# One graph and mixer layer on one core: centring moved to GpSimd, small constants moved behind the last tile, the mixing matrix made by halves

## What is computed

```python
xn  = layernorm(x)
xt  = xn @ weight                                  # graph branch: 4 heads of 64
alpha = softmax(leaky_relu(al[src] + ar[dst]))     # first N edges only
gnn = repeat(sum_h alpha[:, h] * xt[dst][:, h], 4)
q, k, v = split(xn @ w_qkv.T)                      # mixer branch: 8 heads of 64
k, v = instance_norm(k), instance_norm(v)
dots = k.T @ v                                     # per head, 64 x 64, over all rows
mix  = (q @ dots / N) @ w_out.T + b_out
x = x + gnn + mix
x = x + moe(layernorm(x))                          # router, top 2 of 6 experts, 3 layers each
```

## Time and profile before

| what | value |
|---|---|
| median of 3 runs | 802.78 us (802.03 to 805.83) |
| profiled execution | 807.41 us |
| its span, first to last instruction | 805.6 us |
| mean granted TensorE clock | 0.936 of full speed |
| busy: PE, DVE, ACT, POOL | 84%, 69%, 55%, 50% |

### The profile page before, as it was taken

One profiled execution on the slowest core, in us unless ns is written; L12 is line 12 of the kernel. 1 busy time (PEld: TensorE's weight loads), 2 busy tenths in 40 slices (PEclk: granted clock), 3 DMA queues, 4 the chain that ended last, 5 costly groups with the idle time before them and its releaser, 6 DMA issues.

```text
span 805.6 us, 15446 instructions
## 1 busy us (share of the span) xinstructions
PE 679.5 (84%) x4744; PEld 625.0 (78%) x4744; DVE 557.4 (69%) x1401; ACT 442.0 (55%) x873; POOL 398.9 (50%) x439
## 2 busy tenths in 40 slices
PE   3867999999999678878861599999994799999992
PEld 2867888888888567777741499999994799999992
DVE  5676579898888557767746277677773377777772
ACT  2545566777777236756740466556651566565640
POOL 3436378877666000443637045555555145555553
PEclk9989999999999799999955699999998699999997
DMA  8784645444443434764234434343432524545420
GB/s 230 158 166 119 158 126 142 134 126 140 128 121 87 155 118 143 238 191 155 71 99 129 121 117 140 130 140 133 131 120 84 166 88 127 147 124 137 134 73 29
DMA packets 72463, 106.24 MB, mean 132 GB/s; under 512 B 24612, under 2 KB 45605, under 8 KB 72386
## 3 DMA queue, kind: packets, MB, share of 16 engines
q1 hardware_dynamic: 51074, 72.57, 31.9%
q0 software_dynamic: 21312, 32.69, 13.4%
HBM read 60.32 MB, written 46.78 MB: 133 GB/s over the span
## 4 chain that ended last, share of the span: by engine, by line
PE 76%; ACT 6%; DVE 5%; DMA 4%; issue 4%; POOL 3%; SPq 1%; POOLq 0%; DVEq 0%; ACTq 0%
PE kv_ps L1303 10%; PE kv_ps L1305 10%; PE kv_ps L1304 10%; PE pt L1295 6%; PE d_ps L1174 5%; PE kv_ps L1151 5%; PE kv_ps L1154 4%; PE kv_ps L1152 4%; PE kv_ps L1238 3%; PE xt_ps L1295 3%; POOL tab L553 2%; PE pt L1229 2%; PE pt L1154 2%; PE pt L1151 2%; PE pt L1152 2%
## 5 line engine op out<-in xcount | busy, mean ns | idle before, releaser
L1303 PE MATMUL kv_ps<-we_h,now_h 128*128 x648 | 198.1, 306 | 13.9 <-issue 8.3
L1305 PE MATMUL kv_ps<-we_h,now_l 128*128 x648 | 185.5, 286 | 0.0
L1304 PE MATMUL kv_ps<-we_l,now_h 128*128 x648 | 184.9, 285 | 0.0
L1303 PEld LDWEIGHTS kv_ps<-we_h,now_h 128*128 128x128 f32 x648 | 125.6, 194 | 19.6 <-issue 19.6
L1304 PEld LDWEIGHTS kv_ps<-we_l,now_h 128*128 128x128 f32 x648 | 125.4, 194 | 0.0
L1305 PEld LDWEIGHTS kv_ps<-we_h,now_l 128*128 128x128 f32 x648 | 124.7, 193 | 0.0
L1099 DVE TENSOR_TENSOR work<-kv_ps,be 128x256 f32<-128x256 f32 x216 | 81.6, 419 | 45.0 <-PE kv_ps L1305 41.1
L564 POOL TENSOR_TENSOR arena<-work,arena 128x256 f32<-128x256 f32 x80 | 53.1, 683 | 109.2 <-ACT work L730 109.2
L524 POOL DMA_INDIRECT alg<-al_tab,src_all x50 | 62.1, 1243 | 41.9 <-issue 28.1
L914 DVE TENSOR_REDUCE ss<-xring 125x16 f32<-125x1040 f32 x50 | 61.7, 1234 | 20.3 <-ACT xring L635 17.7
L527 POOL DMA_INDIRECT arena<-xt_tab,dst_all x50 | 61.8, 1236 | 15.2 <-issue 15.2
(11 more groups left out here) (238 smaller groups left out, 1832.1 us busy)
## 6 DMA issues: line engine op xcount, KB each, us to landing
arena<-tab SPq DMA_DIRECT2D x40, 259.0 KB
xring<-in_x SPq DMA_DIRECT2D x26, 224.0 KB
xt_tab<-arena SPq DMA_DIRECT2D x10, 568.8 KB
arena<-tab SPq DMA_DIRECT2D x40, 131.0 KB
we_h<-wt_h SPq DMA_DIRECT2D x6, 768.0 KB
we_l<-wt_l SPq DMA_DIRECT2D x6, 768.0 KB
weight_in<-tab SPq DMA_DIRECT2D x14, 259.0 KB
xring<-in_x SPq DMA_DIRECT2D x5, 560.0 KB
```

The lines of the kernel that those rows point to most:

```text
L1303: pe.matmul(outp, hi[:, c, :], we_h[:, w], start=c == 0, stop=False)
L1304: pe.matmul(outp, hi[:, c, :], we_l[:, w], start=False, stop=False)
L1305: last = pe.matmul(outp, lo[:, c, :], we_h[:, w], start=False, stop=c == KC - 1)
```

## The change

It has four parts.

- **Centring.** VectorE keeps the sum and the multiplication of `centre`; the four additions become `kv_centre` on GpSimd, after tiles 29, 31, 33 and 35, each with a wait on `mean_done`. ScalarE's casts move from pairs 14 and 16 to pairs 17 and 19.
- **Small constants.** `small` moves from pair 20 to behind the last pair. The product of zeros that needs its last two areas moves on TensorE from before the first key product to behind the first value product. VectorE and ScalarE wait for it at tile 2.
- **Diagonal copies.** VectorE copies the diagonal blocks first, then does the two `weights` pieces of the last chunk, and the three `graph` pieces and `graph_rows(0)` after one more step.
- **Mixing matrix by halves.** The four first products go into two banks and signal by pairs; ScalarE scales the first half and VectorE the second; the eight products that follow are run by halves of the sum; the two column blocks of the result lie in banks of their own, and are rounded (ScalarE) and lowered (VectorE) one after the other.

The diff, without the declarations of semaphores:

```diff
-PREP_EPS, PREP_BO, PREP_W = 1, 15, 20
+PREP_EPS, PREP_BO, PREP_W = 1, 13, 18
+        a_ps = [kv_ps[0][:, 2 * D * b:2 * D * (b + 1)].rearrange("p (b n) -> p b n", b=2) for b in range(2)]
+        m_ps = [kv_ps[1][:, 512 * c:512 * c + D] for c in range(KC)]
@@ gpsimd
+            def kv_centre(part):
+                half, c = part // 2, part % 2
+                cols = slice(half * MI, half * MI + MI)
+                kv_v = kv_raw[:, c, cols].rearrange("p (h n) -> p h n", n=MC)
+                pool.wait_ge(mean_done, half + 1)
+                pool.tensor_tensor(kv_v, kv_v, kv_mean[:, c, half * MH:half * MH + MH].unsqueeze(2).to_broadcast([128, MH, MC]),
+                                   ALU.add).then_inc(kv_c, 1)
             for t in range(T):
                 normal(t)
+                if t >= 29 and t % 2 == 1 and t < 37:
+                    kv_centre((t - 29) // 2)
                 if t >= 40 and t % 2 == 1 and t < 48:
                     kv_lower((t - 40) // 2)
@@ scalar
-                if i in (14, 16):
-                    half = (i - 14) // 2
+                if i in (17, 19):
+                    half = (i - 17) // 2
-                    act.wait_ge(kv_c, half + 1)
+                    act.wait_ge(kv_c, KC * (half + 1))
+                if t == 2:
+                    act.wait_ge(dz_done, 1)
             act.wait_ge(a_done, 1)
-            act.activation(a_sb, kv_ps[0][:, :].rearrange("p (b n) -> p b n", b=MI // 128), ACT.Copy,
-                           scale=1.0 / N).then_inc(as_done, 1)
+            act.activation(a_sb[:, 0:2, :], a_ps[0], ACT.Copy, scale=1.0 / N).then_inc(as_first, 1)
             for b in range(2):
                 act.wait_ge(cv_out[b], 16 * ROUNDS)
-            act.wait_ge(m_done, 1)
-            act.activation(mix_h, xt_ps[:, :].rearrange("p (c n) -> p c n", c=KC), ACT.Copy).then_inc(mh_done, 1)
+            for c in range(KC):
+                act.wait_ge(m_done, c + 1)
+                act.activation(mix_h[:, c, :], m_ps[c], ACT.Copy).then_inc(mh_done, 1)
@@ vector
-                link(dve.tensor_scalar(mean_v, mean_v, -1.0 / MC, None, ALU.mult))
-                for c in range(KC):
-                    last = dve.tensor_tensor(kv_v[:, c, :, :], kv_v[:, c, :, :], mean_v[:, c, :].unsqueeze(2).to_broadcast([128, MH, MC]), ALU.add)
-                last.then_inc(kv_c, 1)
+                dve.tensor_scalar(mean_v, mean_v, -1.0 / MC, None, ALU.mult).then_inc(mean_done, 1)
-                if i == 20:
-                    small()
-            dve.wait_ge(prep, PREP_W)
+            small()
-            for q in range(5):
+            dve.wait_ge(dT_done, 1)
+            dve.wait_ge(dots_done, T)
+            d_v = d_ps[:, :].rearrange("p (b n) -> p b n", b=MI // 128)
+            for q in range(2):
+                dve.tensor_copy(dotsT[MC * q:MC * (q + 1), :, MC * q:MC * (q + 1)],
+                                d_v[MC * q:MC * (q + 1), :, MC * q:MC * (q + 1)]).then_inc(dT_done, 1)
+            for q in range(2):
+                piece(CHUNKS - 1, q)
+            dve.wait_ge(a_done, 2)
+            dve.tensor_scalar(a_sb[:, 2:4, :], a_ps[1], 1.0 / N, None, ALU.mult).then_inc(as_done, 1)
+            for q in range(2, 5):
                 piece(CHUNKS - 1, q)
             graph_rows(0)
...
-            dve.wait_ge(mh_done, 1)
-            dve.tensor_tensor(mix_l, xt_ps[:, :].rearrange("p (c n) -> p c n", c=KC), mix_h.bitcast(FP32), ALU.subtract).then_inc(ml_done, 1)
+            for c in range(KC):
+                dve.wait_ge(mh_done, c + 1)
+                dve.tensor_tensor(mix_l[:, c, :], m_ps[c], mix_h[:, c, :].bitcast(FP32), ALU.subtract).then_inc(ml_done, 1)
@@ tensor
-            pe.wait_ge(prep, PREP_W)
-            pe.matmul(d_ps[:, :], vs[2][:, 0:128], ks[2], start=True, stop=False, skip_group_check=True)
...
+                if t == 0:
+                    pe.wait_ge(prep, PREP_W)
+                    pe.matmul(d_ps[:, :], vs[2][:, 0:128], ks[2], start=True, stop=False, skip_group_check=True).then_inc(dz_done, 1)
...
-            for q in range(MI // 128):
-                last = pe.matmul(kv_ps[0][:, q * D:(q + 1) * D], dotsT[:, q, :], woT_sb[:, q, :], start=True, stop=True)
-            last.then_inc(a_done, 1)
+            for b in range(2):
+                for q in range(2):
+                    last = pe.matmul(a_ps[b][:, q, :], dotsT[:, 2 * b + q, :], woT_sb[:, 2 * b + q, :], start=True, stop=True)
+                last.then_inc(a_done, 1)
+            def mix_weights(c, b):
+                for q in (2 * b, 2 * b + 1):
+                    last = pe.matmul(m_ps[c], wq_sb[:, q, c * 128:(c + 1) * 128], a_sb[:, q, :],
+                                     start=q == 0, stop=q == MI // 128 - 1)
+                return last
+            pe.wait_ge(as_first, 1)
+            for c in range(KC):
+                mix_weights(c, 0)
             pe.wait_ge(as_done, 1)
-            for c in range(KC):
-                for q in range(MI // 128):
-                    last = pe.matmul(xt_ps[:, c * D:(c + 1) * D], wq_sb[:, q, c * 128:(c + 1) * 128], a_sb[:, q, :],
-                                     start=q == 0, stop=q == MI // 128 - 1)
-            last.then_inc(m_done, 1)
-            pe.wait_ge(ml_done, 1)
+            for c in range(KC):
+                mix_weights(c, 1).then_inc(m_done, 1)
+            pe.wait_ge(ml_done, KC)
```

More of the change, by code:

```diff
@@ L257, in gps_layer @@
         wg_c, wg_hd, wg_ld = sem("wg_c"), sem("wg_hd"), sem("wg_ld")
-        kv_c, kv_hd, kv_ld = sem("kv_c"), sem("kv_hd"), sem("kv_ld")
+        mean_done, kv_c, kv_hd, kv_ld = sem("mean_done"), sem("kv_c"), sem("kv_hd"), sem("kv_ld")
         bs_done, ag_done, sd_done, fin_done = sem("bs_done"), sem("ag_done"), sem("sd_done"), sem("fin_done")
@@ L265, in gps_layer @@
                                                           sem("pr_done"), sem("sr_done"))
-        rc_done, ks_ready, dots_done = sem("rc_done"), sem("ks_ready"), sem("dots_done")
+        rc_done, ks_ready, dz_done, dots_done = sem("rc_done"), sem("ks_ready"), sem("dz_done"), sem("dots_done")
         g_in = [sem(f"g_in{b}") for b in range(2)]
@@ L271, in gps_layer @@
         cvh_done, cvl_done = sem("cvh_done"), sem("cvl_done")
-        dT_done, a_done, as_done, m_done, mh_done, ml_done = (sem("dT_done"), sem("a_done"), sem("as_done"),
+        dT_done, a_done, as_first, as_done, m_done, mh_done, ml_done = (sem("dT_done"), sem("a_done"), sem("as_first"), sem("as_done"),
                                                               sem("m_done"), sem("mh_done"), sem("ml_done"))
@@ L923, in _ @@
                 dve.wait_ge(rc_done, t + 1)
+                if t == 2:
+                    dve.wait_ge(dz_done, 1)
                 if t >= VB:
@@ L950, in _ @@
             graph_rows(0)
-            dve.wait_ge(dT_done, 1)
-            dve.wait_ge(dots_done, T)
-            d_v = d_ps[:, :].rearrange("p (b n) -> p b n", b=MI // 128)
-            for q in range(2):
-                dve.tensor_copy(dotsT[MC * q:MC * (q + 1), :, MC * q:MC * (q + 1)],
-                                d_v[MC * q:MC * (q + 1), :, MC * q:MC * (q + 1)]).then_inc(dT_done, 1)
-            dve.wait_ge(mh_done, 1)
-            dve.tensor_tensor(mix_l, xt_ps[:, :].rearrange("p (c n) -> p c n", c=KC), mix_h.bitcast(FP32), ALU.subtract).then_inc(ml_done, 1)
+            for c in range(KC):
+                dve.wait_ge(mh_done, c + 1)
+                dve.tensor_tensor(mix_l[:, c, :], m_ps[c], mix_h[:, c, :].bitcast(FP32), ALU.subtract).then_inc(ml_done, 1)
             dve.wait_ge(pool_c, POOL_C)
@@ L1196, in _ @@
             pe.wait_ge(dT_done, 3)
-            for q in range(MI // 128):
-                last = pe.matmul(kv_ps[0][:, q * D:(q + 1) * D], dotsT[:, q, :], woT_sb[:, q, :], start=True, stop=True)
-            last.then_inc(a_done, 1)
+            pe.wait_ge(ks_ready, T)
+            pe.wait_ge(sqv_done, T)
+            for b in range(2):
[7 more added lines that the diff above has]
+                return last
+            pe.wait_ge(vs_ready, T)
+            pe.wait_ge(as_first, 1)
+            for c in range(KC):
+                mix_weights(c, 0)
             pe.wait_ge(as_done, 1)
             for c in range(KC):
-                for q in range(MI // 128):
-                    last = pe.matmul(xt_ps[:, c * D:(c + 1) * D], wq_sb[:, q, c * 128:(c + 1) * 128], a_sb[:, q, :],
-                                     start=q == 0, stop=q == MI // 128 - 1)
-            last.then_inc(m_done, 1)
-            pe.wait_ge(ml_done, 1)
+                mix_weights(c, 1).then_inc(m_done, 1)
+            pe.wait_ge(ml_done, KC)
             def mix(i):
```

## The result

| | before | after |
|---|---|---|
| median of 12 runs | 804.09 us (802.03 to 808.06) | 798.49 us (792.89 to 802.37) |
| ratio, 95% interval | | 0.9918 [0.9897, 0.9940] |
| profiled execution, its span | 807.41 us, 805.6 us | 797.89 us, 795.7 us |
| last dots end / mixing starts | 269.44 / 286.50 | 268.95 / 278.56 |

The account below looks back on a forecast made before the run. TensorE, busy 84%, was taken to lose time in the passage behind stage 2 and at the end of stage 1. Gains of 8.85 + 3.15 = 12.0 us from 802.8 gave 790.8 us, range 786.5 to 796.5.

Parts of the forecast that it names:

- stage 1 net: End of stage 1: gain of 3.6 us less 0.45 us for the product of zeros, 3.15 us (2.5 to 3.8).
- passage: Behind stage 2, from last dots to mixing: TensorE starts the mixing at 277.65 instead of 286.50, gain 8.85 us.
- mixing loop: The loop after the passage, untouched by the diff; the forecast's sum had no term for it.
- If all upstream comes earlier, the store does too: Stage 1: the store releasing ScalarE's table copy ahead of the cast also comes earlier, 1.3 us allowed; gain 4.25 us.
- The centring's upstream saving: Stage 1: VectorE gives up 1.29 us of additions twice, ScalarE some 1.0 us of casts twice; 1.3 us allowed.
- The taken 3.6 us: Stage 1 gain before the product of zeros, taken as the middle between 2.95 and 4.25 us.
- The price of an addition: Each centring addition on GpSimd: taken as 1.3 us, bounded by 0.65 and 2.6 us, hidden in idle time.
- stage 1 gives nothing: Rival, 9%: stage 1 is bound by its transfers and the constants only filled a hole; 794.0 us.
- The rival of the clock: Rival, 18%: TensorE's clock still falls in the passage, about 3 us of the gain is lost; 793.8 us.
- The rival of the loop: Rival, 7%: the mixing loop's first row and bias loads come late, half of 8.85 us is lost; 795.2 us.
- GpSimd as the bound: Rival, 2%: additions and normalisations between tiles 29 and 36 bind; whole gain gone at 5.5 us per addition.
- The thin cover of the constants: End of stage 1: 4.5 us of constants against 5.0 us until TensorE wants the zeros; TensorE waits for any tenths missed.

Follow-up runs that it names:

- e9: Changed kernel with the centring additions back on VectorE and the casts behind pairs 14 and 16; 795.01 us, 0.9926 of the kernel before.
- e14: Changed kernel with casts at pairs 15 and 16 and extra products in TensorE's two waits of the mixing loop; 793.95 us, 0.9870 of the kernel before.
- e16: Kernel before with only the diagonal copies and mixing matrix by halves changed, a second time; 797.57 us, 0.9914 of the kernel before.
- e11: The changed kernel itself, run a third time; 795.73 us, 0.9925 of the kernel before.
- e5: Changed kernel with the casts at pairs 15 and 16 instead of 17 and 19; 794.31 us, 0.9886 of the kernel before.
- e8: Changed kernel with casts at pairs 15 and 16 and extra TensorE products during the wait for the diagonal copies; 794.23 us, 0.9887 of the kernel before.
- e10: Changed kernel with the casts at pairs 15 and 16, a second time; 794.03 us, 0.9899 of the kernel before.
- e3: The changed kernel itself, run a second time; 796.00 us, 0.9912 of the kernel before.

## Why the prediction was wrong

The direction and the order of the passage were right, the size was not. By its own steps, with means over all profiles:

| step | forecast | measured |
|---|---|---|
| stage 1 net | 3.15 us | 1.0 us (268.59 - 267.58) |
| passage | 8.85 us | 7.4 us (16.00 over six - 8.58 over twelve) |
| mixing loop | 0 | -1.4 us (130.9 - 132.3) |
| sum | 12.0 us | 7.0 us; by the medians 5.6, 7.0 and 6.7 us |

- *"If all upstream comes earlier, the store does too": this step of stage 1 failed, and with it the forecast that only GpSimd's queue waits for the late cast.* I had named the danger (the cast moved behind a copy that a store releases) and set bounds of 2.95 and 4.25 us on it, but both assumed that the store lands no later against the rest than before. In the profile after it was issued 1.95 us earlier and released ScalarE 0.8 us later (0.95 us earlier and 0.85 us later in the means from the mark), so the cast ended at 68.4, outside both cases. I allowed 1.3 us for busy transfers; they took it all. And the sum followed the cast to GpSimd alone, while ScalarE's `upper` of the next pair stands behind the same wait and the same cast: TensorE stood for 2.0 to 3.0 us for it in all five profiles of the changed stage 1, and in four of them ran at half clock afterwards. With the casts ahead of the wait stage 1 gains 2.8 us (3.0 from the mark), inside the forecast's bounds (2.5 to 3.8); with them behind it, 1.0 us (0.8 from the mark).
- *The centring's upstream saving was worth nothing that the profiles show.* The taken 3.6 us rested on it in part. The constants alone bring 2.9 us net, near the 3.5 - 0.45 = 3.05 us that the forecast had for a GpSimd whose work stays as it was. The price of an addition was 1.04 us, under the 1.3 us taken. The idle time of GpSimd hid it, as argued, but VectorE's time was not what held the stage; only the median of e9 leaves room for some 1 us.
- *The rival "stage 1 gives nothing"*, given 9%, came nearest to the size (0.8 to 1.0 us net), but not by its reason: the constants were no mere filler of a hole, since moving them alone brings 2.9 us.
- *The passage as built was right; its baseline was mis-sized.* Forecast 8.2 us from last dots to mixing; nine of twelve profiles show 8.18 to 8.20. The old passage was taken as 17.06 us from one execution whose clock stayed low long. Over six profiles it is 14.98 to 17.09, mean 16.00.
- *The rival of the clock* came in three of twelve profiles (after, e14, e16: 9.61, 9.80, 9.76 us), near its 18%. It costs 1.5 us, not 3: in the profile after the clock was back 3.8 us after TensorE's restart (270.03 to about 273.84), sooner than the 5.3 us that I had taken as the least. Even in all executions it would not explain the miss.
- *The rival of the loop*, given 7%, happened with a part of its size (1.4 us, not 4.4) by another mechanism: no load was late, the clock fell there.
- *GpSimd as the bound* came nowhere near 5.5 us per addition.
- The profiled execution of before had a loop of 133.9 us, 3.6 us over the other five with the old passage; this is most of the 4.6 us by which it stood above its median. I had taken that excess out of the base, and the passage's own excess of 1.1 us over the mean of six I left in. Without this profile the loop term is -2.0 us, not -1.4.
- The product of zeros costs about what was said. Stage 2 is 185.95 us with it inside and 185.12 without, and TensorE waits 0.57 us for ScalarE's last copy where the 0.86 us of the product had stood: 0.54 us in all, 0.45 forecast. It is in the sums above. The thin cover of the constants held: they end at 84.06, and the product begins at 85.87 without a wait.
- The low end of the range does not follow from its terms: 790.8 - 0.65 - 1 - 0.8 is 788.35 us, not 786.5. That the changed kernel measured 796.0 and 795.7 us later on, just inside the high end, is spread between measurements, not merit of the forecast.

By the prediction's own test, last dots less than 2 us earlier would prove it wrong; they came 0.5 us earlier (at most 3.0 us, in e11, where the drift ahead of the mark made up 1.9), while the mixing came within 10 us behind them.

The best version is the changed kernel with the casts at pairs 15 and 16 (794.0 to 794.3 us, 8.4 to 8.8 us below the kernel before measured beside it). Its interval overlaps that of the changed kernel measured beside it (e11); that it came out lower in all four forms run (e5, e8, e10, e14), and the profiles, speak for it.

## What to carry to other kernels

Moving a step behind an instruction that waits for a transfer gives that step the transfer's timing; an earlier issue was not an earlier landing here, with the DMA engines 93% busy. Follow the wait through the queue of the engine that waits, too: everything behind the moved step is delayed by the wait and by the step. So place what others wait for ahead of such a wait, even if its inputs barely allow it. Read a wait that depends on the clock from several executions before its length becomes a term of a sum, and do not count on a shortened or filled wait to save a fall of the clock: here the fall came elsewhere.

## What the runs showed of the hardware

A small VectorE instruction that met GpSimd's addition lasted as long as the addition. In the profile after, VectorE's `nmr` at 49.91 took 1.02 us and ended with the addition that GpSimd began at 49.87; before, without the addition, it took 0.17 us. The rows of after and of before:

```profile
49.91 1.02 DVE L804 SCALAR_TENSOR_TENSOR nmr<-mv,rs 125x5 f32<-125x5 f32 x1
```

```profile
51.88 0.17 DVE L789 SCALAR_TENSOR_TENSOR nmr<-mv,rs 125x5 f32<-125x5 f32 x1
```

Here VectorE's instruction ends at 50.93, the addition at 50.91. The same instruction took 1.02 us in all eleven profiles with the additions on GpSimd and 0.17 us in all seven without. The Trainium skill's page "SBUF — State Buffer" (SBUF: two separate sides) says that VectorE, when it reads two tensors from SBUF, and GpSimd lock one pair of ports for a whole instruction, and that the loser is blocked; these two rows agree. That next to nothing came of moving the additions may have to do with it; no run here tells.

The rounding of the bias took 0.82 and 0.54 us before, beside a busy GpSimd, and behind the last tile 0.28 us each:

```profile
72.37 0.82 DVE L839 CAST bo_hl<-weight_in 1x256 fp32r<-1x256 f32 x1
73.23 0.54 DVE L840 CAST bo_hl<-weight_in 1x256 fp32r<-1x256 f32 x1
```

```profile
81.70 0.28 DVE L851 CAST bo_hl<-weight_in 1x256 fp32r<-1x256 f32 x1
82.02 0.28 DVE L852 CAST bo_hl<-weight_in 1x256 fp32r<-1x256 f32 x1
```

So the block of constants is 3.4 us long where it now stands (80.65 to 84.06), not 4.49 us. And one program, one wait of 1.08 us and the same work before it gave the clock at 1.00 in e3 and a fall to 0.50 in the profile after: the Trainium skill's page "TensorE: Matmul & The Clock Gate" (What's actually happening) says that the moment is not tied to the program, and these runs agree.
